# Softmax sums of an attention unit: copied over the rows of a head and inverted by VectorE in four parts, in place of two transfers and a 100x20 reciprocal

## The reference, cut to what matters

```python
scores = jnp.einsum('bhqd,bhkd->bhqk', Q, K) * scale
attn = jax.nn.softmax(scores, axis=-1)
out = jnp.einsum('bhqk,bhkd->bhqd', attn, V)
out = out.transpose(0, 2, 1, 3).reshape(B, S, D)
return out @ Wo.T + bo
```

## Time and profile before

| | before |
|---|---|
| median of 3 runs | 2288.55 us (2286.79 to 2288.61) |
| the profiled execution, its own time | 2287.75 us |
| its span, first to last instruction | 2286.0 us |
| ScalarE busy | 2128.7 us, 93% |
| TensorE matmul busy | 2074.4 us, 91% |
| VectorE busy | 971.2 us, 42% |
| GpSimd busy | 390.6 us, 17% |
| granted TensorE clock, mean | 0.981 of full speed |

### The profile page before, as it was taken

The page is one execution under the profiler, slowest core; times in us unless marked ns, Lnnn a source line. Parts: engine busy times, 40 slices in busy tenths (PEclk is TensorE's granted clock), DMA queues, the critical chain, the costliest instruction groups (busy, mean ns, idle before and its releaser), DMA issues.

```text
span 2286.0 us, 123455 instructions
## 1 busy us (share of the span) xinstructions
PE 2074.4 (91%) x56576; PEld 868.6 (38%) x56576; DVE 971.2 (42%) x2291; ACT 2128.7 (93%) x2346; POOL 390.6 (17%) x637
## 2 busy tenths in 40 slices
PE   4798999899998999989999899989999899998885
PEld 2432444344433344334443344434443344433223
DVE  5344334452445434453345533445244542433115
ACT  2499999999999999999999999999999999998994
POOL 2212102130112201131011310213011220111003
PEclk7899999999999999999999999999999999999998
DMA  2312121222111211221121212122211121122001
GB/s 72 82 38 54 40 61 36 59 53 51 47 50 49 64 44 42 57 66 44 49 56 37 71 41 61 37 59 53 51 48 49 50 54 47 41 60 53 19 10 37
DMA packets 115906, 113.92 MB, mean 50 GB/s; under 512 B 41667, under 2 KB 111862, under 8 KB 115377
## 3 DMA queue, kind: packets, MB, share of 16 engines
q1 hardware_dynamic: 112520, 103.85, 17.9%
q10 hardware_dynamic: 2856, 2.08, 0.4%
HBM read 55.16 MB, written 36.86 MB: 40 GB/s over the span
## 4 chain that ended last, share of the span: by engine, by line
ACT 65%; PE 16%; issue 8%; DVE 3%; SPq 3%; POOL 2%; DMA 1%; DVEq 1%; POOLq 0%; ACTq 0%
ACT prob L592 65%; PE PS L1077 6%; PE PS L1047 4%; PE PS L969 2%; SPq L304 2%; PE PS L999 1%; DMA thin<-Osb 1%; SPq L340 1%; PE PS L949 1%; POOL Hs L450 1%; PE PS L1024 1%; PE PS L984 1%; DVE HL L691 0%; DVE HL L689 0%; DVE z L667 0%
## 5 line engine op out<-in xcount | busy, mean ns | idle before, releaser
L592 ACT ACTIVATE prob<-PS 125x1000 f32<-125x1000 f32 x2304 | 2076.6, 1090 | 72.3 <-PE PS L1047 70.3
L1077 PE MATMUL PS<-prob,Vst 64*17 64x500 f32 (+1 forms) x18432 | 1192.0, 580 | 0.7 <-DVE Hs L758 0.6
L1047 PE MATMUL PS<-QA,KA 64*32 64x500 f16 (+1 forms) x18432 | 935.7, 378 | 121.0 <-ACT prob L592 108.8
L1047 PEld LDWEIGHTS PS<-QA,KA 64*32 64x32 f16 (+1 forms) x18432 | 265.1, 90 | 1084.9 <-ACT prob L592 1054.8
L1077 PEld LDWEIGHTS PS<-prob,Vst 64*17 64x17 f32 (+1 forms) x18432 | 334.6, 93 | 33.8 <-issue 7.5
L458 POOL TENSOR_TENSOR sq<-HL 128x500 bf16<-128x500 f16 x96 | 97.9, 1020 | 960.7 <-DVE HL L691 960.7
L689 DVE TENSOR_SCALAR HL<-PS,b_qk 128x500 f16<-128x500 f32 x90 | 66.5, 739 | 445.7 <-PE PS L969 445.7
L969 PE MATMUL PS<-zT,w_qk 64*32 64x250 f32 x5760 | 236.4, 384 | 20.5 <-DVE HL L691 14.5
L465 POOL TENSOR_TENSOR Y<-Hs,be_ln 125x256 f32<-125x256 f32 x96 | 70.2, 731 | 467.0 <-DVE Hs L758 467.0
L999 PE MATMUL PS<-w_o,oT 64*32 64x128 f32 (+1 forms) x6144 | 125.5, 272 | 17.8 <-DMA oT<-Osb 8.2
L969 PEld LDWEIGHTS PS<-zT,w_qk 64*32 64x32 f32 x5760 | 100.0, 107 | 97.7 <-PE PS L969 32.9
(11 more groups left out here) (88 smaller groups left out, 943.3 us busy)
## 6 DMA issues: line engine op xcount, KB each, us to landing
qk_halves_scratch<-HL SPq DMA_DIRECT2D x96, 250.0 KB, 2.3
QA<-qk_halves_scratch SPq DMA_DIRECT2D x384, 62.5 KB
KA<-qk_halves_scratch SPq DMA_DIRECT2D x380, 62.5 KB
oT<-Osb SPq DMA_DIRECT2D x384, 31.2 KB, 2.3
out<-Y SPq DMA_DIRECT2D x23, 448.0 KB
X<-in_x SPq DMA_DIRECT2D x16, 234.4 KB
thin<-Osb SPq DMA_DIRECT2D x96, 7.8 KB
Den<-thin SPq DMA_DIRECT2D x96, 7.8 KB
```

What stands on the lines that cost most here:

```text
L592: act.activation(prob[0:T, 2 * (w % 6):2 * (w % 6) + 2, :], PS[0:T, 2 * (w % 2):2 * (w % 2) + 2, 0:QC], ACT.Exp, scale=scl)\
L1047: last = pe.matmul(PS[lo:hi, bank, 0:QC], KA[rows, G % NG, h // 2, t * T + lo:t * T + hi], QA[rows, G % NG, h // 2, c * QC:(c + 1) * QC], ...
L1077: last = pe.matmul(PS[lo:lo + HD + 1, bank + r, 0:QC], Vst[rows, b % 2, t, g * HG + j, :], prob[rows, (HG * t + j) % 12, :], start=(t == 0 ...
```

## The change

The two transfers and `thin` are gone. After `take_sums`, VectorE copies the row of sums (row 16 of each head, lane `HD`) to all 32 rows of the head and takes the reciprocal on all 128 rows, in four parts of 125 columns, in periods 4, 8, 12 and 16. The multiplication moves from period 14 to period 18, and with it SyncE's store of the attended rows; reloads, the loading of `X` and output stores move from period 15 to period 19. After the last unit, the four parts follow one another behind output tile 5.

```diff
-    TAKE, INVERT, NORMALISE = 1, 9, 14
+    TAKE, INVERT, NORMALISE = 1, (4, 8, 12, 16), 18
+    PARTS = len(INVERT)
...
-            def spread_sums(n):
-                sp.wait_ge(s_ov, at(s_ov, n + 1))
-                sp.dma_start(thin[:, :], Osb[HD:128:2 * HD, :].rearrange("j (s c) -> j s c", s=25)).then_inc(s_pk, 16)
-
-            def gather_sums(n):
-                sp.wait_ge(s_rc, at(s_rc, n + 1))
-                sp.dma_start(Den[0:128:2 * HD, :].rearrange("j (s c) -> j s c", s=25), thin[:, :]).then_inc(s_up, 16)
...
-                        if k == TAKE and n > 0:
-                            spread_sums(n - 1)
-                        if k == INVERT and n > 0:
-                            gather_sums(n - 1)
...
-            def invert(n):
-                dve.wait_ge(s_pk, at(s_pk, 16 * (n + 1)))
-                dve.reciprocal(thin[:, :], thin[:, :]).then_inc(s_rc, 1)
-
-            def normalise(n):
-                dve.wait_ge(s_up, at(s_up, 16 * (n + 1)))
-                dve.stream_shuffle(Den[:, :], Den[:, :], [0] * (2 * HD))
+            def invert(j):
+                lo, hi = j * QC // PARTS, (j + 1) * QC // PARTS
+                dve.drain()
+                dve.stream_shuffle(Den[:, lo:hi], Osb[:, lo:hi], [HD] * (2 * HD))
+                dve.drain()
+                dve.reciprocal(Den[:, lo:hi], Den[:, lo:hi])
+
+            def normalise():
                 dve.drain()
                 dve.tensor_tensor(Osb[:, :], Den[:, :], Osb[:, :], ALU.mult).then_inc(s_on, 1)
...
-                    if k == INVERT and n > 0:
-                        invert(n - 1)
+                    if k in INVERT and n > 0:
+                        invert(INVERT.index(k))
...
-                        invert(B * NU - 1)
+                        for j in range(PARTS):
+                            invert(j)
```

More of the change, by code:

```diff
@@ L205, in audio_tower @@
         Den = sb("Den", [128, QC])
-        thin = sb("thin", [HG * 25, QC // 25])
         oT = sb("oT", [128, KC, NC + 1, QC])
@@ L244, in audio_tower @@
             "s_wsq", "s_top", "s_root", "s_scl", "s_sq", "s_nm", "s_nm1", "s_rerun", "s_flag"))
-        s_sc, s_ex, s_pv, s_ov, s_pk, s_rc, s_up, s_on, s_os = (sem(n) for n in (
-            "s_sc", "s_ex", "s_pv", "s_ov", "s_pk", "s_rc", "s_up", "s_on", "s_os"))
+        s_sc, s_ex, s_pv, s_ov, s_on, s_os = (sem(n) for n in (
+            "s_sc", "s_ex", "s_pv", "s_ov", "s_on", "s_os"))
         s_ms, s_mx, s_wsum = sem("s_ms"), sem("s_mx"), sem("s_wsum")
@@ L267, in audio_tower @@
             s_stp: sum(len(OFFSETS[key[0]]) - 1 for key, use in USE.items() if use >= FIRST or key[0] == "tok"),
-            s_ov: per_unit, s_pk: 16 * per_unit, s_rc: per_unit, s_up: 16 * per_unit, s_on: per_unit, s_os: 64 * per_unit,
+            s_ov: per_unit, s_on: per_unit, s_os: 64 * per_unit,
             s_s1: per_tile, s_r3: per_tile, s_y: per_tile, s_yst[0]: STORED[0], s_yst[1]: STORED[1],
@@ L377, in run @@
                                 stored.append((pb, i))
-                spread_sums(B * NU - 1)
-                gather_sums(B * NU - 1)
                 store_attended(B * NU - 1)
@@ L611, in _ @@
                 dve.memset(Vst[:, b, :, :, HD:HD + 1], 1.0)
-            dve.memset(Den[:, :], 1.0)
             def two(use, rows, cols):
@@ L821, in unit @@
                         take_sums(n - 1)
-                    if k == INVERT and n > 0:
-                        invert(n - 1)
+                    if k in INVERT and n > 0:
+                        invert(INVERT.index(k))
                     if k == NORMALISE and n > 0:
-                        normalise(n - 1)
+                        normalise()
                     if b + 1 < B and (u, k) in STATS:
@@ L893, in run @@
                     if e == CT + 2:
-                        normalise(B * NU - 1)
+                        normalise()
                 finish_out(B - 1, NT - 1)
```

## The result

| | before | after |
|---|---|---|
| median | 2288.58 us (4 runs, 2286.79 to 2291.0) | 2388.23 us (4 runs, 2387.73 to 2394.61) |
| span of the profiled execution | 2286.0 us | 2386.1 us |
| granted TensorE clock, mean | 0.981 | 0.966 |

The changed kernel takes 1.0441 times as long, 95% interval 1.0421 to 1.0461: 99.65 us more. The direction and the range held; the sum of 80 us was 20 us short.

What follows compares the result with a forecast made beforehand. The prediction took ScalarE's exponentials, busy 93% of the span, as the bound, with time growing where scores come late. Its terms summed to 85 us, less some 5, so 2287.75 + 80 = 2368 us, range 2322 to 2402.

Steps and rivals of the forecast that it cites:

- What a part costs: On VectorE, shuffle and reciprocal of 125 columns with gaps: 1.45 us by the upper bound taken, 0.88 by the lower.
- The rival of the cheap reciprocal: On VectorE, a part costs only 0.88 us, giving 2327 to 2335 us; chance 10%.
- Unit 3 into 4: Late store delays unit 4's `take_sums` by 3.45 us; with 1.3 us of clock, 4.7 us in 7 recordings: 33 us.
- Units 4 and 5: Parts delay transposes and the flag, deepening ScalarE's stalls: 10.5 us in unit 4 and 6 us in unit 5.
- Units 9 to 11: Late `take_sums` into unit 10, 8 us; late value piece in unit 10, 12; parts ahead of unit 11's pieces, 8.
- The end: After the last units: multiplication 2.8 us later, then four parts replacing the sums' round trip, 4.8 us more: 7.6 us.
- less some 5 us: Deduction from the sum: ScalarE loses 0.15 us less than TensorE at each of 35 new or deeper stalls.
- The GELU term: ScalarE's stall behind GELU at the start of unit 4, from the late store: 33 us over 7 recordings.
- SyncE's moved queue at no cost: In SyncE's queue, the moved store, reloads and loads cost no stall of their own.
- VectorE falls behind for whole stretches: Rival: lateness carries from unit to unit and costs clock, +115 us or more, 2403 us; chance 7%.
- The rival on the other side: Unit 5's queued sums' transfer and two landings at the end were the price: 11 us gained, 2277 us; chance 5%.
- Its condition: The faster rival decides only if unit 3's multiplication ends by 442.95, with a tokenising piece running behind it.

Runs made afterwards that it cites:

- e4_no_recip: The changed kernel without its 384 reciprocals, the rows multiplied by their sums: 2328.84 us, 1.018 times the kernel before.
- e9_unit3_ahead: The changed kernel with unit 3's multiplication alone moved to period 16, ahead of the second tokenising piece: 2345.58 us, 1.024 times the kernel before.
- e2_store_from_den: The changed kernel with the product written to and stored from `Den`, so `take_sums` doesn't wait for the store: 2322.98 us, 1.0146 times the kernel before.
- e1_early: The changed kernel with parts in periods 3, 6, 8, 10 and multiplication, store and reloads back in 14 and 15: 2347.04 us, 1.0251 times the kernel before.
- e5_one_block: The changed kernel with one part of 500 columns in period 9 and the multiplication back in 14: 2387.13 us, 1.0414 times the kernel before.
- e7_end_only: The kernel before, with four parts instead of the two transfers only after the last unit: 2291.73 us, 1.0004 times the kernel before.
- e11_den_no_recip: The changed kernel with the product stored from `Den` and without its reciprocals: 2297.66 us, 1.0039 times the kernel before.
- e3_move_only: The kernel before with only the multiplication, store and reloads moved to periods 18 and 19, both transfers kept: 2383.31 us, 1.0405 times the kernel before.
- e10_split_reload: The kernel before with unit 4's second 8 reloads issued behind the sums' transfer, in unit 5's period 2: 2283.48 us, 0.9964 times the kernel before.

## Why the prediction was right, and where it was too small

**What a part costs** held at the upper bound: reciprocal 940 ns (966 taken, lower bound 397), shuffle 302 (290), and from one part's start to the next 1.41 us where nothing waits between (1.45). VectorE's 1356.5 us busy were predicted as 1359. With 20 columns at 273 ns, 125 at 940 and 500 at 3278, a column costs 6.35 and 6.2 ns; fixed are some 0.15 us. The estimate of 1.15 us for 125 columns from the Trainium skill (VectorE: DVE Perf Modes, "Walkthrough: the 8-slice pipeline in each mode"), whose repeat count of 8 I had read as 8 cycles a column, is not borne out: it gave 8.3 ns a column. The rival of the cheap reciprocal falls by the 940 ns; e4_no_recip, 2328.84 us, is what leaving the reciprocals out altogether would give.

**Unit 3 into 4**, 33 us: the mechanism is right, and in the recording that was followed the lateness too (3.42 us for 3.45); e9_unit3_ahead and e2_store_from_den show it from two sides. The term was too small, 41.8 us, and the clock is the part of it that was mis-sized. I charged 1.3 us a recording for one projection, 9.1 in all; the two projections together took 14.8 us more. The idle came to 25.8 us where 24.2 were charged, and 1.2 us are left unexplained.

**Units 4 and 5**, 16.5 us: too large, 10.0 measured. In the change parts two and three start in VectorE's waits on GpSimd and end before them, as predicted (1.53 us and 2.38). That this cover doesn't hold two parts, or one block, is shown by e1_early and e5_one_block.

**Units 9 to 11**, 28 us: 19.8 measured. The start of unit 10 was underrated (10.5 for 8), its end overrated (9.1 for 12), and unit 11, 8 us, has next to no loss (0.2). The store that lands late behind unit 11 shows at the start of unit 0 instead, 3.6 us, for which the sum had nothing. The clock, which was to be lower behind these stalls, was so at the start of unit 10 in one of six recordings only, behind 2.72 us of idle; in the other five the idle was 1.27 to 1.68 us and the clock 1.00.

**The end**, 7.6 us: 8.9 measured, 3.3 in ScalarE's last stall and 5.6 behind it. e7_end_only shows the second of its two steps, 4.6 us.

**The term that failed** is "less some 5 us", that ScalarE loses 0.15 us less than TensorE at each stall. In recording 1 behind GELU, TensorE lost 3.42 + 1.73 + 0.44 = 5.6 us and ScalarE 5.9, so there was nothing to take off there. And the sum had nothing for exponentials that no longer overlap or wait for less than 0.15 us, 12.5 + 3.1 us.

**How the sum came within 20 us** is in part luck. The GELU term, the 5 us, the exponentials, the short waits, the start of unit 0 and the end together were 34 us too low; units 4 and 5 and 9 to 11 were 15 us too high.

**SyncE's moved queue at no cost** was right for the change, since the transfer that would have been queued behind it is gone; e11_den_no_recip keeps the moved queue and is 7.4 us over in all. It was nothing to carry over to e3_move_only, which kept that transfer: 35 us.

**VectorE falls behind for whole stretches**: not borne out. e1_early has VectorE busy for 1348.5 us, the change for 1356.5, and it is 41 us faster by the order alone.

**The rival on the other side**, faster by 11 us: of its two halves the queue is real (e10_split_reload, -0.36%; unit 5's stalls fell by 3.9 us, where 6 x 1.26 = 7.6 were counted), and the two landings at the end are a loss of 4.6 us instead. Its condition, a multiplication of unit 3 that ends early enough, was not sufficient: e1_early meets it and stays 2.5% behind, e9_unit3_ahead meets it but for a wait of 0.68 us and stays 2.4% behind.

**What stays open:** what sets the clock behind a given idle. Behind 1.83 to 1.86 us the first projection took 3.00 us in three of the seven recordings of e4_no_recip and 3.86 to 4.73 in the other four; behind 3.10 us or more in the change it was never under 4.21. And of the 34 us of e2_store_from_den its trace places 9.1 at the end of unit 10, 6.1 in the rest of unit 4, 3.4 in the last stall, 5.9 behind it and 8.6 in the exponentials' own time; no run separates them.

## What to carry to other kernels

An engine at 42% is not free: price its additions by what stands behind them in its list, up to the next instruction that a full engine waits for, and write both lists down to the microsecond, as here for unit 3. Before moving an instruction whose result a transfer reads, look up who overwrites the transfer's source, since the landing is added to every delay; storing from a tensor that is overwritten later took 66 of 100 us away. And when steps move together (a multiplication, the reloads, the loads), ask for each queue what now stands ahead of the small transfer that somebody waits for.

## What the runs showed of the hardware that I had not expected

- Behind an idle of 3.42 us TensorE's granted clock stayed at 0.50 for 12 us, across two groups of 64 matmuls with 1.81 us of idle between them. A late start cost 5.6 us at 3.4 us of lateness in this recording, and over all seven 40.5 us at 25.8 us of idle. Behind 1.8 us of idle the same group took anything from 3.00 to 4.73 us (e4_no_recip).
- An exponential of 125x1000 behind any wait takes 1.00 us, where in a row each adds 0.90. Waits too short to be counted as stalls cost this as well: with 12 more stalls than before, e2_store_from_den has 8.6 us more busy time of exponentials.
- The reciprocal's time grows with its columns in a straight line from 20 to 500, at 6.2 to 6.35 ns each, which is more than five times the shuffle's (1.14 ns from 125 to 500 columns).
